# Output rows stored tile by tile by indirect DMAs from POOL, in place of block stores from SP

## The chip, the cores and the metric

The kernel runs on one core of one Trainium2 chip, in one launch. The time is the device time of an execution in microseconds (us); for the kernel before it is the median of 3 runs. The profile is of one further execution.

## What is computed

The reference is a chain of four sublayers over x of shape (2, 2048, 128), all in fp32. Each adds to x the layer norm of its output: `x = x + layernorm(f(layernorm(x)))`. The four f are a local attention with 16 heads, an attention with one shared key head together with a mixture of 8 experts, a causal attention with 2 query heads, and a second mixture. The change is in the last one:

```
logits = x @ router_W + router_b
w, idx = top_k(logits, 2);  gates = one_hot(idx) weighted by softmax(w)
h = layernorm(x) * ln_g + ln_b                       # for each of 8 experts
y = gelu(h @ W1 + b1) @ W2 + b2 + x                  # 128 -> 512 -> 128
out = sum over the experts of y * gates
x = x + layernorm(out)                               # this is what is stored
```

## The kernel before, in words

The 4096 rows of x stay in SBUF for the whole kernel as `X`, 32 tiles of 128 rows (tile t holds rows 128 t to 128 t + 127, one row on each partition, 512 bytes a row). The last stage is `ffn_layer1`. Its rows are worked on in 8 blocks (`NBLK`) of 512 rows, that is 4 tiles (`BPT`) a block. For each block the 8 experts are gone through one after the other; a pair of block and expert is an item, and there are 64 (`ITEMS`).

Each engine has its own queue of instructions, written by hand, and waits on semaphores:

- TensorE (`up`, `down`) makes the four parts of the hidden layer of item j + 1 between the four parts of the second product of item j. Each fp32 product is done as three products of split operands (lines 64 to 66).
- ScalarE (ACT) applies gelu (line 2235) and copies the high part of three of the four parts (line 2241).
- VectorE (DVE) subtracts to get the low part (`low`, line 2352), casts the fourth high part (`high`, line 2358), and scales the product of an item by its gates (`scale`, line 2372). In between it does the closing norm of earlier blocks in small steps (`finish`): `residual` (2377), `total` (2384), `row_stats` (1491 to 1496), and `apply` (1504 and 1508), which writes the finished row tiles into `X`. `F.added` counts these, and `F.applied(n, s)` is its value when tile s of block n is finished.
- POOL adds the scaled product to the accumulator of the block (line 2269), for each item but the first of a block, and once a block takes the power -1/2 of the variances (`F.pool`, line 1512). DVE's `scale` waits for the add of two items earlier, and TensorE turns a finished accumulator back (`turn_back`, line 2495) during the next block.
- SP issues every DMA: the loads of weights at the start of the stage (lines 2174 to 2177), one load of gates an item into one of four buffers (line 2196), one store of turned gates a block (line 2187), and the stores of the output (`store`, line 2182).

An output store moves a whole block: 4 tiles, 256 KB, from `X` to rows of `out`. `STORE_AT = (2, 6)` puts the store of block n in SP's queue at item 6 of block n + 2. The stores of blocks 6 and 7 stand at the end of the queue, and SP then waits until all eight are landed.

`POWER_AT = (1, 4)` puts the power of block n at item 4 of block n + 1 in POOL's queue; that of block 7 stands behind the loop. After the last matmuls of block 7 come, one after the other, the add on POOL, the turning back, the row statistics of its four tiles, the power, `apply` for its four tiles, and the store.

Of the kernel before, what the change touches and what calls it, by code (L numbers as in the profile page):

```python
# [8 lines left out]
U32 = mybir.dt.uint32  # L9
# [4 lines left out]
P = 128  # L14
# [3 lines left out]
TILES = BATCH * SEQ // P  # L18
BT = SEQ // P
BLK = 512  # L20
BPT = BLK // P
NBLK = BATCH * SEQ // BLK
# [2057 lines left out]
GB = 4  # L2080
GATE_AT = 3
KEEP_AT = 7
STORE_AT = (2, 6)
POWER_AT = (1, 4)
APPLY = (10, 12)
FINISH_AT = 2 * (NE + 2)
# [2 lines left out]
def ffn_layer1(nc, dr, X, g, out):  # L2089

    with Mem(nc, "d_") as m:
# [5 lines left out]
        b2 = m.sb("b2", [P, NE])  # L2097
        wr = [m.sb(f"wr{k}", [P, P], F32R) for k in range(2)]
        rbias = m.sb("rbias", [P, NE])
# [15 lines left out]
        lt = m.sb("lt", [32, GRP, BLK])  # L2115
        router = Router(m, g, lg, gate, softmax_first=False)
        late = m.sb("late", [P, NE, FF])
        w2raw = late.rearrange("p e (c d) -> p e c d", d=D)
        gb, accT, tmp = late[:, 0:GB, :], late[:, GB:GB + 2, :], late[:, GB + 2:GB + 4, :]
        a = raw[:, 0:FC, :]  # L2120
# [2 lines left out]
        F = FinishNorm(m, by_rows=True)  # L2123
# [6 lines left out]
        c_in = m.sem("c_in")  # L2130
# [33 lines left out]
        stored = m.sem("stored")  # L2164
# [4 lines left out]
        with nc.Block() as block:  # L2169
            @block.sync  # L2170
            def _(sp):
                for dst, src in ((raw[:, :, :], "d_w1"), (lng[:, :], "d_lng"), (lnb[:, :], "d_lnb"),
                                 (rr[:, :], "d_wr"), (b1raw[:, :, :], "d_b1")):
                    sp.dma_start(dst, dr[src]).then_inc(w_in, 16)
                for dst, src in ((b2[:, :], "d_b2"), (rbias[:, :], "d_rbias")):
                    sp.dma_start(dst, dr[src]).then_inc(c_in, 16)
                sp.dma_start(w2raw[:, :, :, :], dr["d_w2"]).then_inc(w2_in, 16)
                sp.wait_ge(w2_lo, NE)

                def store(n):  # L2180
                    sp.wait_ge(F.added, F.applied(n, BPT - 1))
                    sp.dma_start(out.rearrange("(t p) d -> p t d", p=P)[:, n * BPT:(n + 1) * BPT, :],
                                 X[:, n * BPT:(n + 1) * BPT, :]).then_inc(stored, 16)

                def keep_gates(n):
                    sp.wait_ge(gT_done, n + 1)
                    sp.dma_start(dr["d_gates"][n], gT[:, n % 2, :]).then_inc(gT_out, 16)

                keep_gates(0)
                for j in range(ITEMS):  # L2190
                    n, e = divmod(j, NE)
                    if e == 0:
                        sp.wait_ge(gT_out, 16 * (n + 1))
                    if j >= GB:
                        sp.wait_ge(scaled, j - GB + 1)
                    sp.dma_start(gb[:, j % GB, :], dr["d_gates"][n, e].partition_broadcast(P)).then_inc(gb_in[j % GB], 16)
                    if e == KEEP_AT and n + 1 < NBLK:
                        keep_gates(n + 1)
                    if e == STORE_AT[1] and n >= STORE_AT[0]:
                        store(n - STORE_AT[0])  # L2200
                for n in range(NBLK - STORE_AT[0], NBLK):
                    store(n)
                sp.wait_ge(stored, 16 * NBLK)

            @block.scalar
            def _(act):
# [49 lines left out]
            @block.gpsimd  # L2256
            def _(pool):
                stats_pool(nc, pool, S)
                for e in range(NE):
                    pool.wait_ge(w2_hi, e + 1)  # L2260
                    nc.gpsimd.tensor_tensor(w2l[:, e, :, :], w2raw[:, e, :, :], w2h[:, e, :, :].bitcast(F32),
                                            ALU.subtract).then_inc(w2_lo, 1)
                for j in range(ITEMS):
                    n, e = divmod(j, NE)
                    if e > 0:
                        pool.wait_ge(scaled, j + 1)
                        if e > 1:
                            pool.wait_ge(added, n * (NE - 1) + e - 1)
                        nc.gpsimd.tensor_tensor(accT[:, n % 2, :], accT[:, n % 2, :], tmp[:, e % 2, :],  # L2269
                                                ALU.add).then_inc(added, 1)  # L2270
                    if e == POWER_AT[1] and n >= POWER_AT[0]:
                        F.pool(nc, pool, n - POWER_AT[0], S)
                for n in range(NBLK - POWER_AT[0], NBLK):
                    F.pool(nc, pool, n, S)

            @block.vector
            def _(dve):
# [55 lines left out]
                hidden_bias()  # L2333
                weights(range(NE // 2))
                dve.wait_ge(inv_step, 2)
                dve.wait_ge(c_in, 16 * 2)
                logits(0)
                low(GRP)
                weights(range(NE // 2, NE))
# [84 lines left out]
            def _(pe):  # L2424
# [29 lines left out]
                        last.then_inc(lt_mm, 1)  # L2454
                pe.wait_ge(l_scaled, NBLK)
                pe.wait_ge(lo, 1 + NE)
                pe.wait_ge(c_in, 16 * 2)

                def turn_gates(n):
                    pe.wait_ge(summed, 1)  # L2460
# [40 lines left out]
                for j in range(ITEMS):  # L2501
                    n, e = divmod(j, NE)
# [23 lines left out]
def host_layout(a):  # L2526

    f = np.float32
    z = {}

    z["ident"] = np.eye(P, dtype=f)
    z["identb"] = np.eye(P, dtype=f).astype(mybir.dt.np(BF16))
    cos, sin = rope_tables(SEQ, DH0, 1)
    sin = sin * np.where(np.arange(DH0) % 2 == 0, 1.0, -1.0).astype(f)[:, None]
    z["cs0"] = np.tile(np.stack([t.reshape(DH0, SEQ // SUB, SUB) for t in (cos, sin)], axis=2), (2, 1, 1, 1))
    row = np.arange(P)[:, None] % SEG
    col = np.arange(KEYS0)[None, :]
    masked = np.where((col < PM) | (col - PM <= row), 0.0, -1e30)
    z["mask0"] = np.tile(masked, (1, 4)).astype(mybir.dt.np(BF16))

    z["x"] = a["L0_attn_seq"].reshape(-1, D)
    z["norm_w"] = a["L0_attn_norm_w"].reshape(D, 1)
    z["w_qkv"] = a["L0_attn_w_qkv"]
    z["w_out"] = a["L0_attn_w_out"].reshape(PAIRS, P, D).transpose(1, 0, 2)
    z["b_out"] = np.broadcast_to(a["L0_attn_b_out"], (P, D))
    pk, pv = a["L0_attn_pm_k"], a["L0_attn_pm_v"]
    pmk = np.zeros((P, PAIRS, KEYS0), f)
    pmv = np.zeros((P, PAIRS, P), f)
    for h in range(H0):
        rows = slice((h % 2) * DH0, (h % 2 + 1) * DH0)  # L2550
        pmk[rows, h // 2, 0:PM] = pk[h].T
        slot = (h % 2) * 4 + h % 8 // 2
        pmv[rows, h // 2, slot * PM:(slot + 1) * PM] = pv[h].T
    z["pmkT"], z["pmvT"] = pmk, pmv

    wq, wkc, wvc = a["L0_ffn_Wq"].T, a["L0_ffn_Wkc"].T, a["L0_ffn_Wvc"].T
    z["b_wq"] = np.concatenate([wq[:, h * DK:(h + 1) * DK] for h in range(HB) for _ in range(3)], axis=1)
    z["b_wkv"] = np.concatenate([wkc, wkc, wkc, wvc], axis=1)
    z["b_wr"] = np.pad(a["L0_ffn_Wr"].T, ((0, 0), (0, P - NE)))
    z["b_w13"] = np.concatenate([  # L2560
        np.concatenate([a["L0_ffn_eW" + k].transpose(2, 0, 1), a["L0_ffn_sW" + k].T[:, None, :]], axis=1)
        .reshape(D, -1) for k in "13"], axis=1)
    z["b_g12"] = np.stack([a["L0_ffn_g1"], a["L0_ffn_g2"]], axis=1)
    z["b_w2"] = np.concatenate([a["L0_ffn_eW2"].transpose(2, 0, 1), a["L0_ffn_sW2"].T[:, None, :]], axis=1)
    z["b_wo"] = a["L0_ffn_Wo"].T
    z["b_ebias"] = np.broadcast_to(a["L0_ffn_expert_bias"], (P, NE))
    z["iota"] = np.broadcast_to(np.arange(NE, dtype=f), (P, NE))

    cos, sin = rope_tables(SEQ, D, 2)
    z["cs1"] = np.stack([t.reshape(D, BB, BLK) for t in (cos, sin)], axis=2)  # L2570
    z["mask1"] = np.where(np.arange(P)[None, :] <= np.arange(P)[:, None], 0.0, -1e30).astype(mybir.dt.np(BF16))
    z["c_wkq"] = np.stack([a["L1_attn_Wk"].T] + [a["L1_attn_Wq"][h].T for h in range(HC)], axis=1)
    z["c_wv"] = a["L1_attn_Wv"].T
    z["c_wo"] = a["L1_attn_Wo"].T.reshape(HC, D, D).transpose(1, 0, 2)

    z["d_w1"] = a["L1_ffn_W1"].transpose(1, 0, 2)
    z["d_lng"], z["d_lnb"] = a["L1_ffn_ln_g"].T, a["L1_ffn_ln_b"].T
    z["d_wr"] = np.pad(a["L1_ffn_router_W"], ((0, 0), (0, P - NE)))
    z["d_b1"] = a["L1_ffn_b1"].reshape(NE, FC, P).transpose(2, 0, 1)
    z["d_w2"] = a["L1_ffn_W2"].reshape(NE, FC, P, D).transpose(2, 0, 1, 3)  # L2580
    z["d_b2"] = a["L1_ffn_b2"].T
    z["d_rbias"] = np.broadcast_to(a["L1_ffn_router_b"], (P, NE))
    return {k: np.ascontiguousarray(v) for k, v in z.items()}
# [26 lines left out]
```

## Time and profile before

| what | value |
| --- | --- |
| median of 3 runs (lowest, highest) | 2413.66 us (2410.56, 2414.38) |
| the profiled execution, its own time | 2415.43 us |
| its span, from the first to the last instruction | 2413.6 us |
| mean granted TensorE clock | 0.925 of full speed |
| busy over the span: TensorE, DVE, ACT, POOL | 84%, 73%, 45%, 32% |
| output stores | 8 issues on SP, 256 KB each, 3.7 us median from issue to landing |

A row of the profile gives the start of an instruction in us from the start of the span, its duration, its engine, the line of the kernel, what it writes and reads, and in brackets how long the engine was idle before it and which engine released it. Names have the prefix of their stage, md_ for the last one (mg_X is `X`). md_late holds the gate buffers, the accumulators and the scaled products; md_al and md_ah are the low and high parts of the hidden layer.

### The profile page before, as it was taken

To read this page: it belongs to the slowest core of one execution; us is meant where nothing else is said; L and a number is where in the kernel's file an instruction comes from. 1 tells how busy PE (TensorE), PEld (TensorE's weight loads), DVE (VectorE), ACT (ScalarE), POOL (GpSimd) and SP (SyncE) were. 2 spreads that over 40 slices of the span, in tenths; PEclk is the share of its full clock that TensorE was granted. 3 is DMA by queue.
4 is the path that set the end of the run, shared out by engine and by line. 5 is a ranking of instruction groups with operands and counts; after the bars stand their busy time and mean duration, and the time that the engine had idled before them with its cause. 6 is when DMAs were issued, how large, how long until landed. Compare 5 with 4: busy or idle time off the path is not lost. (4 is left out here: it accounts for less than half of the span.)

```text
span 2413.6 us, 43884 instructions
## 1 busy us (share of the span) xinstructions
PE 2024.6 (84%) x15704; PEld 1563.4 (65%) x15704; DVE 1752.5 (73%) x4054; ACT 1095.3 (45%) x2191; POOL 772.7 (32%) x473
## 2 busy tenths in 40 slices
PE   3888888884799998999858885789779967999997
PEld 2677777763456654666547764678668855777775
DVE  5777777775777737777467777777677776788887
ACT  1555455443255552555532222233223324777775
POOL 3555555552145551555400002200110022222232
PEclk9999999997699996999979997899889977999999
DMA  4111111111000000000000001000000010111111
GB/s 158 71 71 62 63 62 71 63 71 37 0 1 2 1 1 1 1 1 2 1 0 0 0 0 42 1 1 1 1 1 1 1 72 29 47 50 54 54 52 37
DMA packets 44164, 71.56 MB, mean 30 GB/s; under 512 B 8320, under 2 KB 18176, under 8 KB 43200
## 3 DMA queue, kind: packets, MB, share of 16 engines
q1 hardware_dynamic: 43968, 68.96, 8.3%
q8 instruction: 121, 1.98, 0.4%
q14 instruction: 75, 0.61, 0.1%
HBM read 33.15 MB, written 2.23 MB: 15 GB/s over the span
## 5 line engine op out<-in xcount | busy, mean ns | idle before, releaser
L1047 POOL TENSOR_TENSOR mb_psum<-mb_pt 128x1024 f32<-128x1024 f32 x112 | 266.8, 2385 | 313.6 <-ACT mb_pt L1027 312.5
L1027 ACT ACTIVATE mb_pt<-mb_stb 128x1024 f32<-128x1024 f32 x256 | 249.2, 1021 | 147.1 <-PE mb_stb L1128 146.6
L915 DVE TENSOR_REDUCE mb_mxp<-mb_p1b 128x1 f32<-128x512 f32 x352 | 231.4, 685 | 65.7 <-PE mb_p1b L1112 61.9
L2352 DVE TENSOR_TENSOR md_al<-md_raw,md_ah 128x512 fp32r<-128x512 f32 x256 | 194.9, 770 | 69.1 <-ACT md_ah L2241 65.4
L351 DVE TENSOR_TENSOR ma_tr<-ma_pbank,ma_cs 128x512 f32<-128x512 f32 x256 | 161.8, 684 | 89.5 <-PE ma_pbank L66 81.6
L2235 ACT ACTIVATE md_raw<-md_bk,md_b 128x512 f32<-128x512 f32 x256 | 174.0, 685 | 68.2 <-PE md_bk L66 68.1
L1951 ACT ACTIVATE mc_p<-mc_sb,mc_nb 128x512 f32<-128x512 f32 (+3 forms) x160 | 98.1, 621 | 188.8 <-DVE mc_nb L1839 188.8
L2269 POOL TENSOR_TENSOR md_late<-md_late 128x512 f32<-128x512 f32 x56 | 93.2, 1665 | 278.2 <-DVE md_late L2372 278.2
L488 ACT ACTIVATE ma_e<-ma_sbank,ma_mx 128x80 f32<-128x80 f32 x512 | 120.8, 387 | 97.7 <-DVE ma_mx L358 97.7
L2029 PE MATMUL mc_pv<-mc_v,mc_pt 128*128 128x128 f32 x1088 | 150.1, 282 | 11.6 <-DVE mc_pt L1888 11.4
L1112 PE MATMUL mb_p1b<-mb_ks,mb_qs 96*128 96x512 f32 x352 | 151.7, 475 | 6.7 <-DVE mb_qs L908 2.8
L2029 PEld LDWEIGHTS mc_pv<-mc_v,mc_pt 128*128 128x128 f32 x1088 | 134.1, 193 | 23.0 <-DVE mc_pt L1888 18.8
L1128 PE MATMUL mb_stb<-mb_qs,mb_ks 98*128 98x512 f32 x512 | 144.5, 403 | 0.8 <-ACT mb_pt L1027 0.8
L439 POOL TENSOR_TENSOR ma_qt<-ma_tr,ma_swp 128x512 f32<-128x512 f32 x64 | 83.4, 1305 | 168.8 <-DMA ma_swp<-ma_tr 160.4
L1139 PE MATMUL mb_pvb<-mb_pt,mb_v 128*32 128x256 f32 x2048 | 136.9, 385 | 0.0
L1512 POOL TENSOR_TENSOR mc_frs<-mc_fve,mc_half 128x4 f32<-128x4 f32 x8 | 8.1, 1009 | 377.1 <-DVE mc_fve L1496 377.1
L915 DVE TENSOR_REDUCE mb_mxp<-mb_misc 128x1 f32<-128x512 f32 x160 | 109.4, 684 | 21.9 <-PE mb_misc L1112 21.9
L2241 ACT ACTIVATE md_ah<-md_raw 128x512 fp32r<-128x512 f32 x192 | 119.2, 621 | 0.0
L1385 ACT ACTIVATE mb_s<-mb_ub 128x512 f32<-128x512 f32 x72 | 43.0, 599 | 164.4 <-PE mb_ub L66 164.4
L1829 DVE TENSOR_REDUCE mc_mp<-mc_sb 128x1 f32<-128x512 f32 (+3 forms) x160 | 96.7, 609 | 28.0 <-PE mc_sb L2008 14.4
L1128 PEld LDWEIGHTS mb_stb<-mb_qs,mb_ks 98*128 98x128 f32 x512 | 94.6, 190 | 33.4 <-issue 12.3
L498 ACT ACTIVATE ma_pt<-ma_fbank 128x512 f32<-128x512 f32 (+1 forms) x160 | 94.4, 591 | 40.7 <-PE ma_fbank L605 40.2
(343 smaller groups left out, 5417.2 us busy)
## 6 DMA issues: line engine op xcount, KB each, us to landing
ma_swp<-ma_tr SPq DMA_DIRECT2D x256, 128.0 KB, 2.0
md_late<-d_gates SPq DMA_DIRECT2D x64, 256.0 KB, 3.2
mg_X<-x SPq DMA_DIRECT2D x4, 512.0 KB, 9.7
ma_cs<-cs SPq DMA_DIRECT2D x1, 2048.0 KB, 9.9
mc_cs<-cs SPq DMA_DIRECT2D x1, 2048.0 KB, 8.5
md_raw<-d_w SPq DMA_DIRECT2D x1, 2048.0 KB, 7.4
md_late<-d_w SPq DMA_DIRECT2D x1, 2048.0 KB, 10.5
out<-mg_X SPq DMA_DIRECT2D x8, 256.0 KB, 3.7
```

Source lines behind the costliest of these rows:

```text
L351: nc.vector.tensor_tensor(tr[:, G % TRS, part, :, :], pbank[:, i % 2, :].rearrange("p (c t) -> p c t", c=2), cs[:, b // 2, part, None, :]. ...
L488: nc.scalar.activation(e[:, s, slot, :], sbank[:, 2 * j + k // 4, k % 4 * KEYS0:(k % 4 + 1) * KEYS0], ACT.Exp, bias=mx[:, s, slot:slot + 1 ...
L915: nc.vector.tensor_reduce(mxp[:, r // NCH, r % NCH:r % NCH + 1], pass_bank(r), AXX, ALU.max).then_inc(p1_max, 1)
L1027: nc.scalar.activation(pt[:, T % RING, :, :].rearrange("p (b h) q -> p b (h q)", b=2), stb[:, 2 * (i % 2):2 * (i % 2) + 2, :], ACT.Exp, sc ...
L1047: nc.gpsimd.tensor_tensor(psum[:, n % SUMS, :, :], pt[:, T % RING, :, :], pt[:, (T + 1) % RING, :, :], ALU.add).then_inc(summed, 1)
L1112: nc.tensor.matmul(pass_bank(r), qs[V % 3][0:QROWS, h, t * P:(t + 1) * P], ks[0:QROWS, c * BLK:(c + 1) * BLK], start=True, stop=True).then ...
L1128: last = nc.tensor.matmul(stb[:, 2 * (i % 2) + hp, :], ks[:, i * P:(i + 1) * P], qs[U % 3][:, 2 * hp:2 * hp + 2, :].rearrange("p h q -> p ...
L1139: last = nc.tensor.matmul(pvb[h * DK:(h + 1) * DK, 0:UQ], v1[:, i, :], pt[:, T % RING, h, :], start=(i == 0), stop=(i == KT - 1), skip_gro ...
L2029: last = nc.tensor.matmul(pv[:, 0:D], pt[:, k % 2, a * P:(a + 1) * P], v[:, c * BPT + a, :], start=(c == 0 and a == 0), stop=(c == chunks[ ...
L2235: nc.scalar.activation(a[:, c, :], ub[:, c, :], ACT.Gelu, bias=b1[:, e, c:c + 1]).then_inc(gelu, 1)
L2241: nc.scalar.activation(ah[:, c, :], a[:, c, :], ACT.Copy).then_inc(hi_act, 1)
L2352: nc.vector.tensor_tensor(al[:, c, :], a[:, c, :], ah[:, c, :].bitcast(F32), ALU.subtract).then_inc(lo_done, 1)
```

## The change

The stage gets a small tensor of row numbers, `rows`, 128 partitions by 32 columns of 32-bit integers: column t holds, on partition p, the number 128 t + p. It is loaded at the start of the stage with the two loads that `c_in` counts, so those who wait for `c_in` now wait for three loads (DVE, TensorE, and also POOL ahead of its loop).

The block stores are gone from SP's queue, with its last wait. POOL issues one indirect DMA for each tile: source is the tile in `X` (64 KB), and the row of `out` to which each partition's row goes is read from the tile's column of `rows`. There are 32 of them. `STORE_AT = 3`: at items 0 to 3 of block n, for n from 3 on, POOL issues the four stores of block n - 3, each ahead of that item's accumulator add. The stores of blocks 5, 6 and 7, twelve in all, stand at the end of POOL's queue behind the power of block 7, in order of block and tile. POOL then waits until all 32 are landed.

```
-STORE_AT = (2, 6)
+STORE_AT = 3
...
+        rows = m.sb("rows", [P, TILES], U32)
...
-                for dst, src in ((b2[:, :], "d_b2"), (rbias[:, :], "d_rbias")):
+                for dst, src in ((b2[:, :], "d_b2"), (rbias[:, :], "d_rbias"), (rows[:, :], "rows")):
                     sp.dma_start(dst, dr[src]).then_inc(c_in, 16)
                 sp.dma_start(w2raw[:, :, :, :], dr["d_w2"]).then_inc(w2_in, 16)
                 sp.wait_ge(w2_lo, NE)
-
-                def store(n):
-                    sp.wait_ge(F.added, F.applied(n, BPT - 1))
-                    sp.dma_start(out.rearrange("(t p) d -> p t d", p=P)[:, n * BPT:(n + 1) * BPT, :],
-                                 X[:, n * BPT:(n + 1) * BPT, :]).then_inc(stored, 16)
...
-                    if e == STORE_AT[1] and n >= STORE_AT[0]:
-                        store(n - STORE_AT[0])
-                for n in range(NBLK - STORE_AT[0], NBLK):
-                    store(n)
-                sp.wait_ge(stored, 16 * NBLK)
...
+                def store(n, s):
+                    tile = n * BPT + s
+                    pool.wait_ge(F.added, F.applied(n, s))
+                    nc.gpsimd.indirect_dma_start(out[:, :], bass.IndirectOffsetOnAxis(ap=rows[:, tile:tile + 1], axis=0),
+                                                 X[:, tile, :], None).then_inc(stored, 16)
+
+                pool.wait_ge(c_in, 16 * 3)
                 for j in range(ITEMS):
                     n, e = divmod(j, NE)
+                    if n >= STORE_AT and e < BPT:
+                        store(n - STORE_AT, e)
                     if e > 0:
                         pool.wait_ge(scaled, j + 1)
...
                 for n in range(NBLK - POWER_AT[0], NBLK):
                     F.pool(nc, pool, n, S)
+                for n in range(NBLK - STORE_AT, NBLK):
+                    for s in range(BPT):
+                        store(n, s)
+                pool.wait_ge(stored, 16 * NBLK * BPT)
...
-                dve.wait_ge(c_in, 16 * 2)
+                dve.wait_ge(c_in, 16 * 3)
...
-                pe.wait_ge(c_in, 16 * 2)
+                pe.wait_ge(c_in, 16 * 3)
...
+    z["rows"] = np.arange(TILES * P, dtype=np.uint32).reshape(TILES, P).T
```

## Rows read from the trace of the kernel before

**Rows 1.** Stretches: bounds, length, busy (count) PE PEld DVE ACT POOL, clock, DMA share, GB/s.

```profile
2182.00:2228.00 46.00, 45.56 (x201) 36.39 (x200) 37.93 (x74) 34.22 (x58) 13.20 (x8) 1.00 0.16 53
2398.00:2413.60 15.60, 0.66 (x5) 0.42 (x4) 9.50 (x30) 0.00 (x0) 2.37 (x3) 0.65 0.12 34
```

**Rows 2.** The chain that ended last, in the tail: start, us, what.

```profile
2398.88 1.29 POOL md_late L2269
2406.29 1.05 POOLq L2169
...
2409.50 0.29 DVE mg_X L1508
```

**Rows 3.** SP's output stores: issues, last landing, DMA movement behind it, end.

```profile
2373.90 0.44 SPq L2182 DMA_DIRECT2D out<-mg_X  x1
...
2400.94 9.27 SPq L2182 DMA_DIRECT2D out<-mg_X  x2
...
L2182 SPq DMA_DIRECT2D out<-mg_X x1: 388/388/388, 2409.8 to 2409.8; - x1
DMA to landing us min/median/max: 2.3/2.3/2.3
...
2410.40:2411.00 0.60, 0.00 (x0) 0.00 (x0) 0.00 (x0) 0.00 (x0) 0.00 (x0) 0.50 0.39 114
2411.00:2412.00 1.00, 0.00 (x0) 0.00 (x0) 0.00 (x0) 0.00 (x0) 0.00 (x0) 0.50 0.70 194
...
L2169 SPq COMPARE_BRANCH  x1: 33/33/33, 2412.1 to 2412.1; - x1
```

**Rows 4.** POOL's groups by shape: count, busy us, mean ns, idle before.

```profile
L2269 POOL TENSOR_TENSOR md_late<-md_late 128x512 f32<-128x512 f32 x56 | 93.2, 1665 | 278.2 <-DVE md_late L2372 278.2
L457 POOL TENSOR_TENSOR ma_yr<-ma_yve,ma_eps 128x1 f32<-128x1 f32 x32 | 17.5, 546 | 20.4 <-DVE ma_yve L385 20.4
L734 POOL TENSOR_TENSOR md_rs<-md_ve,md_half 128x16 f32<-128x16 f32 x4 | 11.6, 2944 | 6.8 <-DVE md_ve L723 6.8
L1512 POOL TENSOR_TENSOR mc_frs<-mc_fve,mc_half 128x4 f32<-128x4 f32 x8 | 8.1, 1009 | 377.1 <-DVE mc_fve L1496 377.1
L2602 POOL MEMSET const-bfloat16-1.0<- 128x1 bf16 x1 | 0.1, 102 | 0.0
```

**Rows 5.** POOL in order of time: start of the stage, and a block.

```profile
2007.73 9.88 POOL L2261 TENSOR_TENSOR md_w2l<-md_late,md_w2h 128x512 fp32r<-128x512 f32 x8 [27.39 <-ACT md_w2h L2221]
...
2157.71 1.49 POOL L1512 TENSOR_TENSOR md_frs<-md_fve,md_half 128x4 f32<-128x4 f32 x1
...
2183.06 1.67 POOL L2269 TENSOR_TENSOR md_late<-md_late 128x512 f32<-128x512 f32 x1 [9.08 <-DVE md_late L2372]
2188.82 1.66 POOL L2269 TENSOR_TENSOR md_late<-md_late 128x512 f32<-128x512 f32 x1 [4.08 <-DVE md_late L2372]
2196.95 1.67 POOL L2269 TENSOR_TENSOR md_late<-md_late 128x512 f32<-128x512 f32 x1 [6.48 <-DVE md_late L2372]
```

**Rows 6.** Loads at the start of the stage, and who needs them.

```profile
1969.11 0.44 SPq L2176 DMA_DIRECT2D md_rbias<-d_rbias  x1
1969.59 0.61 SPq L2177 DMA_DIRECT2D md_late<-d_w  x1
...
md_rbias<-d_rbias SPq DMA_DIRECT2D x1, 4.0 KB, 6.9
...
2000.71 0.90 DVE L2300 TENSOR_TENSOR md_lg<-md_bk,md_inv 128x32 f32<-128x32 f32 x4 [3.20 <-PE md_bk L2452]
```

**Rows 7.** DVE beside POOL, and the room before TensorE needs its result.

```profile
2157.54 1.28 DVE L2352 TENSOR_TENSOR md_al<-md_raw,md_ah 128x512 fp32r<-128x512 f32 x2
...
2369.19 0.87 DVE L2352 TENSOR_TENSOR md_al<-md_raw,md_ah 128x512 fp32r<-128x512 f32 x1 [0.30 <-ACT md_ah L2241]
...
2371.85 0.39 PE L64 MATMUL md_bk<-md_ah,md_w2h 128*128 128x512 f32 x1
...
2399.09 1.23 DVE L1508 TENSOR_TENSOR mg_X<-mg_X,md_raw 128x128 f32<-128x128 f32 x1
```

## The prediction

> **What bounds the kernel now.** I read four views, from coarse to fine. First the table of stretches over the last stage: in every block of about 46 us TensorE is busy for all but 0.4 us at the full granted clock (1.00, that is 2.4 GHz), DVE for 38 us, POOL for 13 us [rows 1]. Until about 2398 us the stage is set by TensorE alone, and what the change does there matters only if it makes TensorE wait. From 2398 us to the end TensorE has almost nothing; these 15.6 us are a serial tail. So, second, the chain of waits over the tail: the last add on POOL, the turn back and the row statistics of block 7, one POOL instruction (the power, from 2406.29 for 1.05 us, so done at 2407.34), then DVE's four pairs of scale and add until 2409.79 [rows 2]. Third, SP's part: the last block store is issued at 2409.82, takes 0.39 us to issue and lands 2.3 us after its start; SP passes its wait at 2412.1 and the span ends at 2413.6, so 1.5 us are closing work [rows 3]. Fourth, POOL's own instructions by shape and in order of time, because the change puts 32 instructions there [rows 4, 5].
>
> **Part 1, taken away: eight block stores on SP.** Each costs SP 0.39 to 0.44 us of issue [rows 3], and SP is not waited for: it re-loads a gate buffer once its old value is used, four buffers deep, and TensorE shows no gap for it [rows 1]. Gain in the steady part 0. In the tail, what goes is the path 2409.79 to 2412.1 of the last block store.
>
> **Part 2, added to the start of the stage: one load of 16 KB (row numbers) and a count of 3 in place of 2.** SP issues it between rbias (1969.11, landing after 6.9 us, so about 1976) and the raw W2 (1969.59) [rows 6]. The first to need the count is DVE's product with inv at 2000.71, over 20 us later [rows 6]; W2 is issued some 0.45 us later, and is needed (POOL's subtractions, behind ACT's copies) only at 2007.73, 38 us after its issue [rows 5, 6]. Cost 0; with the cover gone it would be 0.5 us. POOL's own wait on that count stands behind its W2 subtractions, which end at 2017.6 [rows 5].
>
> **Part 3, added in the steady part: 20 indirect stores on POOL** (blocks 0 to 4, four each, during blocks 3 to 7). Their wait is on rows finished at least a block earlier, so it doesn't hold. Queued behind each is the next accumulator add; for that add DVE waits two items on and TensorE's turn back a block on. Stores 0 and 1 of a block come between the add of item 7 and that of item 1, where POOL idles 9.08 us; store 2 where it idles 4.08 us; store 3 where it idles 6.48 us [rows 5]. Anything up to 4.08 us a store is hidden, and past that an add is late against a wait that has another item of room.
>
> The less visible cost is on DVE. POOL and DVE hold each other up: alone POOL's add takes 1.29 us (the last one), beside DVE's work 1.67 us [rows 2, 4]; and DVE's 128x128 add took 1.23 us beside POOL's last add, ending 0.15 us after it, where the last such add took 0.29 us [rows 2, 7]. So I let a store hold DVE for its whole length T. TensorE has room for it: the subtraction of part 0 of an item is over at 2370.06 and its product starts at 2371.85, 1.8 us later [rows 7]. With T under 1.8 us the cost is 0. Two stores in a row do not add up if DVE gets in between; the power right behind an add took 1.49 us and not 1.01, and two of DVE's subtractions ran to their end beside it, in 1.28 us, which says that it does [rows 4, 5, 7].
>
> The Trainium skill (SBUF — State Buffer, section "SBUF: two separate sides") says that a DMA issued by POOL can't write its descriptors while DVE runs a two-port operation. Whichever of DVE's instructions those are here, one of the long kind, a subtraction, is over in 0.87 us [rows 7], so by the rule each store would end at most that much later, in gaps of over 4 us: 0 in the steady part, and in the tail at most 0.87 us for each of the three stores that start before DVE is done, 2.6 us. It would not turn the result, and no run here shows it yet.
>
> **Part 4, moved into the tail: 12 stores.** This is where the time comes from. Blocks 5, 6 and 7 have no place in POOL's loop; all their stores stand behind the power of block 7 in POOL's queue. In the kernel before, blocks 5 and 6 left at 2373.90 and 2400.94 [rows 3]. Now POOL starts the first of 12 at 2407.34. The four of block 7 come last, when DVE (done at 2409.79) is long through, even if slowed, since eight stores lie ahead of them. So the end is
>
> 2407.34 + 12 T + L + 1.5.
>
> L, from the end of POOL's last instruction until the 64 KB are landed: the 256 KB store took 2.3 us from the start of issue; its movement was 0.39 of 0.60 us plus 0.70 of 1.00 us of the DMA engines, 0.93 us together [rows 3]; a quarter of the bytes saves 0.70 us, which leaves 1.6 us from the start and 1.2 us from the end of issue. Ends 1.2 and 2.3; I take 1.6, as a list made by POOL may start later. The DMA engines themselves don't bound it: 0.93 us for 256 KB is 0.23 us a store.
>
> T isn't in the trace: there is no DMA issued by POOL. From below, the nearest rows are POOL's memset at 0.10 us and SP's issue at 0.39 us [rows 3, 4]. From above, POOL's 128x16 power at 2.94 us [rows 4]. The power gives POOL's price of software work: 0.546 us for 1 column, 1.009 for 4, 2.944 for 16, so about 0.4 us fixed and 0.155 us (the first step) for each 128 words [rows 4]. A store must make, for 128 rows, an address and a length on both sides, 4 words a row: the work of the 128x4 power, 1.01 us. Looking up the row number is a fifth word: 1.17. I take T = 1.2 us, near the 1.01 row.
>
> Sum: 2407.34 + 14.4 + 1.6 + 1.5 = 2424.8, against a span of 2413.6: +11.2 us. The profiled execution of before took 2415.43 us with 1.8 us around its span, so it would become 2426.6; the median of the runs shown is 1.8 us under the profiled one, so **2424.9 us** for the median. Each 0.1 us on T is 1.2 us on the result. Without L's uncertainty: L = 1.2 gives 2424.5, L = 2.3 gives 2425.6.
>
> **The rivals.**
> (a) *The store is cheap for POOL*, as for SP, 0.43 us: POOL is through at 2412.5 and the end is 2412.5 + 1.6 + 1.5 = 2415.6, +2.0 us: not slower by what can be told (2415.7). At the memset's 0.10 us DVE's 2409.79 binds again and it is 2409.79 + 0.10 + 1.2 + 1.5 = 2412.6, -1.0 us. It decides at T = (4.8 + 3.2) / 12 = 0.67 us. For it: SP issues a whole block in 0.43 us. Against it: POOL needs 0.4 us before any work, and 0.546 us for one word per row. The rule that would bring this about stands in the Trainium skill (DMA: Bandwidth & Descriptors, Anatomy of one DMA): the fixed cost of a DMA issued by POOL is mostly the receipt, and making descriptors is small. Chance 0.12.
> (b) *The store is dear*, T between 1.67 and 2.94 us: 12 x 2.94 - 3.2 = +32 us at its end, 2446; at 1.67 it is +16.8, 2430.5. Above 1.8 us TensorE may also wait, 20 times at most 1.1 us. For it: per-row work that is less parallel than the power's. Chance 0.13.
> (c) *The stores cost TensorE time as well.* If DVE doesn't get in between the item-7 add and the two stores behind it, it is held for 1.67 + 2.4 = 4.1 us, 2.3 us over the room of 1.8; in five blocks that is +11 us on top, 2436. Against it the row of the power, above. Chance 0.08.
> (d) The forecast's mechanism, T from 0.7 to 1.67: 2418.9 to 2430.5. Chance 0.67.
>
> The range is 2417 to 2440: T from 0.54 to 2.46 us without (c), and (c) at T = 1.2. Since 0.2% (4.8 us) is about what a measurement of this kernel can tell from no change, slower takes (b), (c), (d): 0.87; of (a) nearly all is within 0.2%: 0.11, and 0.02 is left for faster, since even a free store has only about 1 us to give.
>
> **What the profile after would show.** Until 2398 us nothing moves: the same 46 us a block, TensorE without gaps, POOL's adds at the same distance. After the power of block 7: twelve stores in a row on POOL, about 1.2 us each, DVE done at about 2409.8 while POOL is at its third, and the chain ending in POOL and not in SP. Step 3 is wrong if DVE's subtractions beside a store run past their room and TensorE's busy share of blocks 3 to 7 falls; step 4 is wrong if T isn't near 1.2 or if the last landing is much over 1.6 us. The forecast as a whole is wrong if the twelve stores take under 8 us.

## The result and the profile after

The changed kernel took 2428.26 us (median of 4 runs, 2424.51 to 2432.84), the kernel before 2413.85 us in the runs made with it (median of 4, 2410.56 to 2414.38). The ratio is 1.0066, 95% interval 1.0048 to 1.0083: slower. Between the two medians it is 14.4 us, a ratio of 1.0060, inside that interval. Forecast were 2424.9 us and a range of 2417 to 2440.

The profiled execution of the changed kernel was the quickest of its four: 2424.51 us, span 2422.7 us. That span can't be held against the 2413.6 us of before as it stands, since the last stage begins at another time in each execution. Two marks inside the stage take this out: the start of POOL's first accumulator add, and the start of the power of block 7. In the kernel before, its first add started at 2044.59 us and the power at about 2406.32 us [rows 2 has the chain's 2406.29]: a *steady stretch* of 361.7 us, and a *tail* of 7.3 us up to the end of the span:

```profile
2044.59 1.67 POOL L2269 TENSOR_TENSOR md_late<-md_late 128x512 f32<-128x512 f32 x1 [26.97 <-DVE md_late L2372]
...
2406.32 1.01 POOL L1512 TENSOR_TENSOR md_frs<-md_fve,md_half 128x4 f32<-128x4 f32 x1 [6.15 <-DVE md_fve L1496]
```

The same marks after, from POOL in order of time (start us, us, engine, line, what), with the twelve stores of the tail shortened to the first two and the last:

```profile
2039.12 1.60 POOL L2269 TENSOR_TENSOR md_late<-md_late 128x512 f32<-128x512 f32 x1 [27.25 <-DVE md_late L2376]
...
2401.04 1.01 POOL L1512 TENSOR_TENSOR md_frs<-md_fve,md_half 128x4 f32<-128x4 f32 x1 [6.40 <-DVE md_fve L1496]
2402.24 1.10 POOL L2257 DMA_INDIRECT out<-mg_X,md_rows  x1 [0.19 <-issue]
2403.65 0.96 POOL L2257 DMA_INDIRECT out<-mg_X,md_rows  x1 [0.30 <-DVE md_raw L1504]
...
2416.28 0.96 POOL L2257 DMA_INDIRECT out<-mg_X,md_rows  x1 [0.31 <-issue]
```

Steady stretch 2401.04 - 2039.12 = 361.9 us; tail 2422.7 - 2401.04 = 21.7 us. The stretch is the same to 0.2 us, the tail is 14.4 us longer, as much as lies between the medians.

Each store has POOL busy for 0.96 us, and 0.30 us more pass before the next; twelve take 2417.24 - 2402.06 = 15.18 us, 1.265 us each. What follows the last one is in the queue's own instructions of line 2170, the end of the stage, and in the landing of the last store:

```profile
L2257 POOL DMA_INDIRECT out<-mg_X,md_rows x1: 959/959/959, 2416.3 to 2416.3; - x1
DMA to landing us min/median/max: 2.2/2.2/2.2
```

```profile
L2170 POOLq COMPARE_BRANCH  x1: 38/38/38, 2418.5 to 2418.5; - x1
L2170 POOLq DRAIN  x1: 2670/2670/2670, 2418.7 to 2418.7; - x1
L2170 SPq EVENT_SEMAPHORE  x1: 17/17/17, 2421.5 to 2421.5; - x1
```

POOL passes its last wait at 2418.5 (before, SP did at 2412.1 [rows 3]) and then drains for 2.67 us, for which the other engines wait until 2421.5. From that last wait to the end of the span it is 4.2 us, where it was 1.5.

The steady part of the stage, by stretches with the columns of [rows 1], has POOL busier by four stores a block and TensorE as full as before:

```profile
2182.00:2228.00 46.00, 45.56 (x200) 36.34 (x199) 38.01 (x73) 34.40 (x57) 18.11 (x12) 1.00 0.17 53
2321.00:2367.00 46.00, 45.56 (x200) 36.35 (x200) 38.03 (x74) 34.88 (x58) 18.10 (x12) 1.00 0.17 53
```

Beside DVE's work a store takes longer than the 0.96 us of the tail. This is the first block with stores on POOL (to be held against [rows 5]), and two of DVE's instructions at the same time:

```profile
2168.65 1.47 POOL L2257 DMA_INDIRECT out<-mg_X,md_rows  x1 [0.17 <-issue]
2170.42 1.22 POOL L2257 DMA_INDIRECT out<-mg_X,md_rows  x1 [0.30 <-issue]
2177.56 1.66 POOL L2269 TENSOR_TENSOR md_late<-md_late 128x512 f32<-128x512 f32 x1 [5.92 <-DVE md_late L2376]
2179.38 1.25 POOL L2257 DMA_INDIRECT out<-mg_X,md_rows  x1 [0.16 <-POOL md_late L2269]
2183.32 1.65 POOL L2269 TENSOR_TENSOR md_late<-md_late 128x512 f32<-128x512 f32 x1 [2.69 <-DVE md_late L2376]
```

```profile
2169.57 0.43 DVE L2362 CAST md_ah<-md_raw 128x512 fp32r<-128x512 f32 x1
2170.12 0.69 DVE L2356 TENSOR_TENSOR md_al<-md_raw,md_ah 128x512 fp32r<-128x512 f32 x1
```

The idle time ahead of the adds shrinks from 9.08 and 4.08 us to 5.92 and 2.69 us and is still there, so no add is late. The DVE subtraction at 2170.12 takes its undisturbed 0.69 us though a store runs beside it from 2170.42.

A block later a cast meets a store and is held a little, and the store behind it is slow without a cast beside it:

```profile
2214.83 1.29 POOL L2257 DMA_INDIRECT out<-mg_X,md_rows  x1 [0.17 <-issue]
2215.76 0.59 DVE L2362 CAST md_ah<-md_raw 128x512 fp32r<-128x512 f32 x1
2216.43 1.41 POOL L2257 DMA_INDIRECT out<-mg_X,md_rows  x1 [0.30 <-issue]
```

None of the 37 such casts between 2180 and 2390 us of the kernel before takes over 0.43 us.

### The profile page after: what moved, and what is told of

It reads as the page before. It is cut to its first block and busy times, and to the rows that moved or that the text cites. A ratio compares the mean times of both kernels' runs of the same rounds, so it can differ in the third digit from the quotient of the medians.

```text
span 2422.7 us, 43910 instructions
## 1 busy us (share of the span) xinstructions
PE 2019.6 (83%) x15704; PEld 1559.0 (64%) x15704; DVE 1750.6 (72%) x4054; ACT 1095.1 (45%) x2191; POOL 809.6 (33%) x505
## 5 line engine op out<-in xcount | busy, mean ns | idle before, releaser
L1128 PEld LDWEIGHTS mb_stb<-mb_qs,mb_ks 98*128 98x128 f32 x512 | 94.6, 190 | 33.5 <-issue 12.4
```

The costliest lines, as they stand in the source:

```text
L1128: last = nc.tensor.matmul(stb[:, 2 * (i % 2) + hp, :], ks[:, i * P:(i + 1) * P], qs[U % 3][:, 2 * hp:2 * hp + 2, :].rearrange("p h q -> p ...
```

## The experiments

All of them are read by the two marks, and by POOL's drain. The last two columns are the ratio to the kernel before in runs on the same chip (95% interval). A dash is a kernel that ran once.

| kernel | DMAs from POOL | steady stretch us | tail us | POOL's drain us | ratio |
| --- | --- | --- | --- | --- | --- |
| before | 0 | 361.7 | 7.3 | hidden | 1 |
| changed | 32 | 361.9 | 21.7 | 2.670 | 1.0066 (1.0048 to 1.0083) |
| e1_sp_tail | 20 | 361.6 | 7.3 | hidden | 0.9999 (0.9989 to 1.0010) |
| e2_tail8 | 32 | 361.7 | 16.6 | 2.670 | 1.0045 (1.0029 to 1.0061) |
| e3_sp_tiles | 0 | 361.7 | 6.6 | hidden | 0.9995 (0.9983 to 1.0006) |
| e4_pool_direct | 32 | 361.9 | 12.9 | 2.667 | 1.0026 (1.0015 to 1.0037) |
| e5_four_behind | 32 | 361.9 | 12.4 | 2.670 | 1.0022 (1.0007 to 1.0037) |
| e6_double_loop | 52 | 361.7 | 23.2 | 4.303 | 1.0068 (1.0043 to 1.0093) |
| e7_last_by_pool | 1 | 361.8 | 8.3 | 0.126 | 1.0005 (0.9996 to 1.0015) |
| e8_half_tiles | 44 | 361.7 | 36.3 | 3.650 | - |
| e9_small_extra | 88 | 361.7 | 26.4 | 7.252 | - |

**Is all of it in the tail?** e1_sp_tail keeps the 20 indirect stores of the loop and gives blocks 5, 6 and 7 back to SP as block stores.

```
-                for n in range(NBLK - STORE_AT, NBLK):
-                    for s in range(BPT):
-                        store(n, s)
-                pool.wait_ge(stored, 16 * NBLK * BPT)
+                pool.wait_ge(stored, 16 * (NBLK - STORE_AT) * BPT)
...                                                        # SP
+                    if e == 6 and n == NBLK - 1:
+                        store(n - 2)
+                for n in (NBLK - 2, NBLK - 1):
+                    store(n)
```

> Only the 20 stores in POOL's loop stay indirect; blocks 5, 6 and 7 leave by block stores from SP, as before. Theory A (all of the 14.4 us is made in the tail: twelve stores at 1.26 us behind the power, and POOL's closing drain of 2.7 us behind the last landing): the tail from the start of the power of block 7 to the end of the span is 7.3 us as before, since the drain now runs beside SP's last store, and the time is that of before, 2413.9, within 2 us. Rival B (the stores in the loop, or the mere use of POOL's DMA queue, cost too): the time stays 4 us or more above before, and the stretch from the first accumulator add to the power of block 7 is longer than 361.7 us by as much.

Theory A: tail 7.3 us, ratio 0.9999. Twenty indirect stores in the loop cost nothing. POOL's drain is there, but beside SP's last store. It begins at once and includes the power (2404.29 to 2405.30), so some 1.7 us are its own; SP passes its wait long after it:

```profile
L2171 POOLq DRAIN  x1: 2611/2611/2611, 2404.4 to 2404.4; - x1
L2171 SPq COMPARE_BRANCH  x1: 33/33/33, 2410.1 to 2410.1; - x1
```

**What is one store in the tail worth?** e2_tail8 is one number, and moves four of the twelve into the loop.

```
-STORE_AT = 3
+STORE_AT = 2
```

> STORE_AT = 2: block 5's four stores move into the loop, eight stay behind the power of block 7. Theory A: the tail falls by 4 x 1.265 = 5.1 us, from 21.7 to 16.6, the time to about 2423.2. Rival C (the tail is set by landing and closing, not by the issue of each store): less than 2 us.

The tail fell by 5.1 us to 16.6: what 4 x 1.265 gives.

**Is it the tile by tile, or POOL, or the list of rows?** e3_sp_tiles stores tile by tile from SP, with STORE_AT = (3, 6); e4_pool_direct leaves out the list only.

```
+                    for s in range(BPT):                     # e3, on SP, in the kernel before
+                        tile = n * BPT + s
+                        sp.wait_ge(F.added, F.applied(n, s))
+                        sp.dma_start(out[tile * P:(tile + 1) * P, :], X[:, tile, :]).then_inc(stored, 16)
...
-                    nc.gpsimd.indirect_dma_start(out[:, :], ...)     # e4, on POOL, in the changed kernel
+                    pool.dma_start(out[tile * P:(tile + 1) * P, :], X[:, tile, :]).then_inc(stored, 16)
```

> The kernel before with 32 direct stores of one tile each from SP in place of 8 of a block, blocks 5 to 7 at the end of SP's queue. Theory A: block 5 and 6 leave before the power of block 7, so only block 7 is behind it; its last 64 KB are issued at the last apply and land in about 1.6 us: tail 6.6 to 7.3 us, time as before or 0.7 us less. Rival D (storing tile by tile is what costs, whoever issues): the time rises by 3 us or more.

> As the changed kernel, but each of POOL's 32 stores is a direct DMA with no list of rows. Theory A (what costs is that POOL makes the lists of descriptors, with or without row numbers): 0.8 to 1.3 us a store in the tail, time 8 us or more above before. Rival E (the list of row numbers is what costs): at most 0.5 us a store, tail at most 12.5 us, time at most 5 us above before.

e3: tail 6.6 us, 0.7 us shorter than before, as a 64 KB store lands sooner than one of 256 KB (1.5 us for the last one, against 2.3); in the time this can't be told from none. Going tile by tile costs nothing, and rival D falls. e4 came out between the two theories: less than A expected, a tail of 12.9 us just above E's 12.5, and a time 4.5 us above before by the medians and 6.3 us by the ratio, on either side of E's 5. Its twelve stores follow one another without a gap in 6.46 us, 0.54 us each:

```profile
2402.93 1.01 POOL L1512 TENSOR_TENSOR md_frs<-md_fve,md_half 128x4 f32<-128x4 f32 x1 [6.39 <-DVE md_fve L1496]
2403.91 6.46 POOL L2257 DMA_DIRECT2D out<-mg_X  x12
```

So of the 1.265 us of an indirect store 0.54 us are what POOL needs for a direct one, and 0.73 us are what the indirect form, with its list of rows, adds (of which 0.30 us are the gap behind each). Both theories were half right: POOL as the issuer costs, and the indirect form costs more.

**Could the order of POOL's queue have avoided it?** e5_four_behind puts block 6's stores ahead of the power of block 7.

```
+                for s in range(BPT):
+                    store(NBLK - 2, s)
+                F.pool(nc, pool, NBLK - 1, S)
+                for s in range(BPT):
+                    store(NBLK - 1, s)
```

> Block 5's stores in the loop (STORE_AT = 2), block 6's between the last add and the power of block 7, only block 7's four behind the power. Theory A (the order of POOL's queue put eight stores on the path that had no need to be there): tail from the start of that power to the end of the span 21.7 - 8 x 1.265 = 11.5 us, time about 2418, if four stores (5.1 us) fit into POOL's idle 6.1 us ahead of the power. Rival F (POOL's stores hold up DVE's row statistics beside them, so the power starts later): the stretch from the first accumulator add to that power grows from 361.7 us by 1 us or more, and the time is 2419 or above.

Rival F falls, though the median of 2419.71 us alone would have met its bound (before took 2414.69 in the same runs): the stretch is 361.9 us with four stores beside DVE's row statistics, ended before the power is due:

```profile
2398.27 0.96 POOL L2257 DMA_INDIRECT out<-mg_X,md_rows  x1 [0.30 <-issue]
2400.63 1.04 POOL L1512 TENSOR_TENSOR md_frs<-md_fve,md_half 128x4 f32<-128x4 f32 x1 [1.40 <-DVE md_fve L1496]
2402.67 1.03 POOL L2257 DMA_INDIRECT out<-mg_X,md_rows  x1 [1.00 <-DVE md_raw L1504]
```

The tail is 12.4 us and not 11.5: the first store behind the power is now block 7's own and waits 1.00 us for DVE to finish that tile; with eight others ahead this wait had been covered. The ratio of 1.0022, 5.3 us, agrees with the 5.1 us that the tail is longer than before. Two thirds of what the tail had gained, 9.3 of 14.4 us, were order.

**Does the loop really have room?** e6_double_loop issues each of its 20 stores twice, the second to a spare tensor.

```
                     if n >= STORE_AT and e < BPT:
                         store(n - STORE_AT, e)
+                        store(n - STORE_AT, e, spare)
```

> The changed kernel with each of the 20 stores in POOL's loop issued a second time, to a spare tensor; the tail is as in the changed kernel. Theory A (the loop's stores are free, covered by POOL's idle time and by TensorE's room): stretch from the first add to the power of block 7 within 0.3 us of 361.7, time as the changed kernel's, 2428, within 2 us. Rival B (each costs TensorE or DVE time that one copy was just able to hide or that noise covered): the stretch grows by 2 us or more.

Stretch 361.7 us with 40 stores in the loop: free. But the tail had grown by 1.6 us, to 23.2, without a store more in it: POOL's drain was now 4.303 us. Theory A, which had the time within 2 us of 2428, missed this: the median was 2432.0 us.

**What is the drain?** e7_last_by_pool is the kernel before with its last block store issued by POOL, one direct DMA. e8_half_tiles cuts the twelve stores of the tail in two, 64 rows each. e9_small_extra adds 56 direct DMAs of 16 rows of 32 bytes to the loop.

```
+                pool.wait_ge(F.added, F.applied(n, BPT - 1))                      # e7
+                pool.dma_start(out.rearrange(...)[:, n * BPT:(n + 1) * BPT, :],
+                               X[:, n * BPT:(n + 1) * BPT, :]).then_inc(last_out, 16)
...
+                        for h in range(2):                                        # e8, blocks 5 to 7
+                            nc.gpsimd.indirect_dma_start(
+                                out[:, :], bass.IndirectOffsetOnAxis(ap=half[:, 2 * tile + h:2 * tile + h + 1], axis=0),
+                                X[h * 64:(h + 1) * 64, tile, :], None).then_inc(stored, 16)
...
+                    if n > 0:                                                     # e9
+                        pool.dma_start(dr["spare"][16 * j:16 * (j + 1), 0:NE], lng[0:16, :]).then_inc(small, 16)
```

> The kernel before, only the last block store (256 KB) is issued by POOL, as one direct DMA, in place of SP. Theory G (once POOL has issued any DMA its closing drain takes 2.7 us, and here it stands behind the landing): tail 3.5 us to DVE's end, 2.3 to 2.7 to land, 4.2 to close, 10.0 to 10.4 us in all; time 3 us above before. Rival H (the drain's length comes from the many indirect stores): drain under 1 us, tail at most 8 us, time within 1 us of before.

> The changed kernel with each of the twelve stores of the tail cut in two indirect stores of 64 rows (24 in all). If a store costs a fixed 0.4 us and the rest by its rows (0.86 us for 128): 0.83 us each, tail 21.7 + 4.8 = 26.5 us. Rival I (all of the 1.265 us is fixed, whatever the rows): tail 36.9 us. Rival J (all of it goes by the rows): 21.7 us.

> The changed kernel with 56 more direct DMAs from POOL inside the loop, one for each item from block 1 on, of 16 rows of 32 bytes each to a spare tensor. Theory K (POOL's closing drain goes by the number of DMAs that POOL has issued, whatever their size or kind, 0.04 us + 0.082 us each, read from 1, 32, 44 and 52 of them): 88 DMAs, drain 7.2 to 7.3 us, tail 21.7 + 4.6 = 26.3 us. Rival L (it goes by the descriptors or bytes, of which these 56 add under a quarter): drain at most 3.3 us, tail at most 22.3 us. Both: the stretch from the first add to the power of block 7 stays within 0.5 us of 361.7.

e7 refuted theory G, that any use of POOL's DMA queue costs the 2.7 us: with one DMA the drain is 0.126 us. The tail is 8.3 us, 0.3 over H's bound: this one DMA of 256 KB keeps POOL busy for 0.95 us, where SP issued the same store in 0.39.

```profile
2408.86 0.95 POOL L2277 DMA_DIRECT2D out<-mg_X  x1 [2.76 <-DVE mg_X L1508]
```

Rival H's form, that it comes from many *indirect* stores, fell with e4, whose 32 direct ones gave 2.667. What is left is the count. The drains of e7, e6, e8 and e9, in this order, for 1, 52, 44 and 88 DMAs:

```profile
L2170 POOLq DRAIN  x1: 126/126/126, 2411.9 to 2411.9; - x1
```

```profile
L2170 POOLq DRAIN  x1: 4303/4303/4303, 2426.7 to 2426.7; - x1
```

```profile
L2171 POOLq DRAIN  x1: 3650/3650/3650, 2437.2 to 2437.2; - x1
```

```profile
L2171 POOLq DRAIN  x1: 7252/7252/7252, 2423.2 to 2423.2; - x1
```

The first four counts (1, 32, 44, 52) lie on 0.04 us + 0.082 us for each DMA that POOL issued; e9 was run to test it, with DMAs of 512 bytes, and gave 7.252 us for the 7.2 to 7.3 expected. Rival L falls. The 20 DMAs of e1 give 1.7 us by it, which is what was read there. Neither size nor kind counts, nor when they ran: the 56 of e9 were issued from 2079.8 to 2397.1 us, and the drain began at 2423.2. POOL's other instructions do not count either. The kernel before has the same adds and powers and no DMA from POOL, and its drain, which begins with the power at 2406.3, ends within 0.1 us of it:

```profile
L2169 POOLq DRAIN  x1: 1111/1111/1111, 2406.3 to 2406.3; - x1
```

e8 also says what a store's 1.265 us is made of. With 64 rows it is 0.90 us busy and 0.30 us gap, 1.20 us: half the rows save 0.065 us. Rival I (all fixed) is right within 5% for a store, and the split of 0.4 us fixed and 0.86 us by rows is wrong. Of the 14.6 us by which the tail grew, the stores are 13.6 and the longer drain 1.0, which no theory had counted.

```profile
L2263 POOL DMA_INDIRECT out<-mg_X,md_half_rows x24: 892/897/1032, 2407.1 to 2434.9; - x24
L2259 POOL DMA_INDIRECT out<-mg_X,md_rows x20: 983/1254/1468, 2173.8 to 2375.0; - x20
```

No version beats the kernel before by what can be measured; e3_sp_tiles is 0.7 us better in the tail.

## Why the prediction was right, step by step

- *Part 1, the stores taken from SP's loop, worth nothing; part 2, the load of row numbers, hidden.* Right: the steady stretch and TensorE's busy time did not move. One of the eight issues from SP took 1.77 us (2189.13), over the 0.39 to 0.44 of the prediction, and SP had room for it. Part 2 was not tried by itself, but the traces bear it out: from SP's first load of the stage to POOL's first accumulator add it is 78.7 to 79.1 us in the three kernels without the row numbers (before, e3, e7), and 76.5 to 79.2 us in the eight with them.
- *Part 3, 20 stores in the loop, hidden.* Right, by e1 and, doubled, by e6. The way there was too dark: I let a store hold DVE for its whole length. The subtraction beside a store took its undisturbed 0.69 us, and a cast 0.59 us for 0.43. The store is held as well: the 16 stores of the loop that met DVE's work took 1.22 to 1.47 us, the four that met none 0.98 to 0.99 us. The rule of the Trainium skill that was weighed (SBUF — State Buffer, section "SBUF: two separate sides") is that a DMA from POOL waits while DVE runs a two-port operation; the 0.5 us at most is within the 0.87 us that the prediction allowed for it. But if the cast is taken for that operation the traces don't bear it out: the store at 2216.43 took 1.41 us with no cast beside it, and in e6 one took 0.96 us though a cast began during it (2189.79, held to 0.58 us). Which of DVE's instructions holds a store stays open. Rival (c) falls.
- *Part 4, twelve stores behind the power.* The mechanism was right, and three terms of the sum were off. T: 1.265 us for 1.2, +0.8 us over twelve. L: 2418.5 - 2417.24, about 1.25 us for 1.6, -0.35 us; the 1.2 us that the prediction had worked out from its rows was right, and the 0.4 us on top of it was not. The closing work: 4.2 us for 1.5, +2.7 us. Together +3.15 us on the +11.2 forecast: 14.35, where 14.4 was measured.
- *The step that failed* is "1.5 us are closing work": it was read from a kernel in which POOL issues no DMA, and carried over as a constant. The drain, 2.67 us, was no term of the sum and in none of the rivals; it is nearly all of the error. The forecast missed the median by 3.4 us.
- *T = 1.2 us was near for a wrong reason.* I counted words by the price of the power. By e4 and e8 it is 0.54 us for a direct store of a tile from POOL and 0.73 us for the indirect form, and the rows weigh little: 0.065 us for 64 of them. That counting words came so near was luck.
- *Rival (a), the cheap store.* The rule behind it in the Trainium skill (DMA: Bandwidth & Descriptors, Anatomy of one DMA) says of one DMA from POOL that its fixed cost is mostly the receipt and that making descriptors is small. It doesn't carry to a row of them: here POOL's issuing is 15.2 us of the tail and the last landing 1.25 us. Even for a single store, POOL is busy for 0.96 of the 2.2 us from issue to landing. Yet e4 shows that a direct store would have been under the 0.67 us from which I said that (a) decides, and it was still slower than before by 1.0026 (1.0015 to 1.0037), because of the drain: without its 2.7 us e4's tail would be 2.9 us over that of before. In the chances, (b), (c) and (d) add up to 0.88 and not to 0.87.

## What to carry to other kernels

Ask what stands ahead of the last transfer in its own queue: here eight stores whose data were ready stood behind an instruction that came late, at 1.27 us each. Moving them ahead of it took 9.3 us off the tail (e5), a direct store in place of the indirect one 8.8 (e4). Inside a loop that leaves POOL idle time a DMA issued by POOL cost nothing but its 0.08 us of drain at the end. It is dear in a tail, where POOL needs 0.54 us for a direct store of 64 KB, 0.95 us for one of 256 KB, and 1.27 us for an indirect one of 128 rows (1.20 us for 64). Closing costs move with the engine: when the last wait goes to another engine, its drain comes onto the path.

## What the runs showed of the hardware that was not expected

POOL's drain at the end of a stage took 0.04 us + 0.082 us for each DMA POOL had issued: 0.126 us for 1, 2.670 for 32, 3.650 for 44, 4.303 for 52, 7.252 for 88, the same for direct and indirect ones (2.667 and 2.670) and for 512 bytes and 64 KB. What the drain does in that time stays open.

Executions of one kernel spread by more than most of the differences studied here: the kernel before ran from 2406.3 to 2418.2 us over 26 runs. In the profiles the steady stretch stays within 361.6 to 361.9 us while the last stage's first add starts anywhere from 2038.69 (e5) to 2047.37 us (e6), so much of the spread is made ahead of the last stage. Marks inside the stage told 0.7 us apart where medians did not.
